# A graph network of two GATv2 layers and an edge attention: one-word sort records, part of them scattered later, and four buffers in the table loop

## The chip, the cores and the metric

The kernel runs on one core of one Trainium2 chip. The metric is the time of one execution in device microseconds (us). The program is one launch; it has no communication with other cores.

## What is computed

The graph has 6250 nodes with 128 features and 100000 edges (`src`, `dst`; `dst` is sorted). Cut to what matters:

```python
def _gatv2(x, edge_index, Wl, bl, Wr, br, att, bias):      # H = 3 heads of 128
    loops = jnp.arange(n)
    src = jnp.concatenate([edge_index[0], loops])
    dst = jnp.concatenate([edge_index[1], loops])
    xl = (x @ Wl + bl).reshape(n, h, d)
    xr = (x @ Wr + br).reshape(n, h, d)
    e = jax.nn.leaky_relu(xl[src] + xr[dst], NEG_SLOPE)
    score = jnp.einsum('ehd,hd->eh', e, att)
    ...
    alpha = ex / denom[dst]                                 # softmax over the edges of one dst
    out = jax.ops.segment_sum(alpha[:, :, None] * xl[src], dst, num_segments=n)

def _L0_gnn_ref(x, ...):
    x_in = _gatv2(x, edge_index, Wl1, ...)
    h = relu(_batchnorm(x_in @ W1 + b1, g1, be1))
    h2 = _gatv2(h, edge_index, Wl2, ...)
    return relu(_batchnorm(concat([h2, x_in]) @ W2 + b2, g2, be2))

def _L1_gnn_ref(embeds, ...):                               # 8 heads of 16
    q, k, v = rows @ qTrans, cols @ kTrans, cols @ vTrans   # rows = embeds[src], cols = embeds[dst]
    att = exp(clip(einsum('ehd,ehd->eh', q, k), -10, 10)); normalised over the edges of one src
    res = segment_sum(att * v, src) + embeds                # then a layer norm

x = x + _L0_gnn_ref(relu(layernorm(x)), ...)
x = x + _L1_gnn_ref(relu(layernorm(x)), ...)
```

The sums over edges run twice by `dst` (the two GATv2 layers) and once by `src` (the edge attention), so the edges are needed in both orders.

## The kernel before

Nodes lie in 49 blocks of 128 (`NB`). Edges are placed into slots so that each tile of 128 slots holds edges of one block alone; a table over the slots then says which row to gather (`gather_col` by `dst`, `gather_src` by `src`) and which node of the block (`lo`, the lane) each slot adds to. All edges are cut into 800 columns of 125 (`COLS`, `EC`). Each engine has its own instruction stream and queue; they meet at semaphores, and a block (`with nc.Block()`) ends with a barrier of all of them. The program is a chain of such stages:

- Constants, loading of the keys, and a counting loop.
- The sort block (`sort_by_dst`). First the rank loop works out the `dst` slot of each column on VectorE, ScalarE and TensorE. GpSimd (POOL) meanwhile writes one record of two words per edge with 800 indirect DMAs, one per column, into DRAM (`Records.write`, L634). After the rank loop the other engines go on without it: the ranks by `src` (`beside.on_vector` and its fellows), then `permute`, which puts the 800 columns into their `src` slots by one-hot products: VectorE makes two one-hots for a column (L795, L797), ScalarE scales the small one by two pieces of the record (L858), and TensorE adds four products of 416 columns to four banks (L837). Then come the load of x (L1010, L1012), a layer norm, and the tables of layer 1 (`table_parts`): 49 times TensorE multiplies a block, ScalarE copies it (L1169), SyncE stores it to `xl_table` (L1135), with two buffers in turn. The block ends when all of this and POOL's scatters are done.
- `slot_tables` reads the `dst` records back and makes the tables by `dst`.
- `gat_edges` of layer 1: 464 groups of two tiles. POOL gathers two times 128 rows of `xl_table` for a group (L1269), TensorE forms products (L1330, L1343), VectorE adds and takes the leaky relu (L1472, L1480), ScalarE sums scores (`reduce`, L1422) and weights rows (`weight`, L1406). The stream of each engine is a hardware loop over 16 groups (`pipeline`, L119), 25 times round in the middle. SyncE loads keys, gates, and an index tile for the gathers (`load_index`, L1288).
- `node_layer`, `batch_norm`, the tables of layer 2, `gat_edges` of layer 2, `node_layer`, `batch_norm` with a second load of x, `residual_tables` (stores to `kv_table`, L1794, four buffers), `edge_attention` (gathers by `gather_src`, L1914), and the end.

One fact of the compiled program, in which an instruction has 64 bytes: ScalarE's loop over 16 groups in `gat_edges` has 313 instructions, at positions 1058 to 1370 of its stream in layer 1 and 1999 to 2311 in layer 2. The functions that the change touches:

Of the kernel before, what the change touches and what calls it, by code (L numbers as in the profile page):

```python
# [5 lines left out]
F32 = mybir.dt.float32  # L6
# [26 lines left out]
MOVE = 8  # L33

PAD_KEY = 16384
# [4 lines left out]
G = 4  # L40
# [10 lines left out]
assert max(T_DST, T_SRC) <= TILES and GROUPS <= 512  # L51
# [87 lines left out]
class Core:  # L139


    def __init__(self, nc, ctx):
# [27 lines left out]
        self.block_row = sb("block_row", [1, TILES // G], I32)  # L170
# [10 lines left out]
        self.rec_d = dram("rec_by_dst", [SLOTS, 2], I32)  # L181
# [34 lines left out]
def constants(k, io, by_src):  # L216
# [4 lines left out]
    fill_d = cut(2 * SLOTROW, I32)  # L221
    node_f, long_i = cut(NB), cut(T_SRC, I32)
    made, filled, order, stored = k.sem("c_iota"), k.sem("c_fill"), k.sem("c_order"), k.sem("c_stored")
    with nc.Block() as block:
        @block.gpsimd
        def _(pool):
# [4 lines left out]
            nc.gpsimd.iota(long_i, pattern=[[1, T_SRC]], base=0, channel_multiplier=0).then_inc(made, 1)  # L231

        @block.vector
        def _(dve):
            do = Order(dve, order)
            do(nc.vector.memset(fill_d, 0))
            nc.vector.memset(fill_d.rearrange("p (s f) -> p s f", f=2)[:, :, 1:2], PAD_KEY).then_inc(filled, 1)
# [13 lines left out]
        @block.sync  # L251
        def _(sp):
            sp.wait_ge(filled, 1)
            sp.dma_start(k.rec_d.rearrange("(p s) f -> p (s f)", p=P), fill_d).then_inc(stored, 16)
            sp.wait_ge(stored, 16)


def sort_by_dst(k, io, beside):
# [23 lines left out]
    self_pos = far(NB, I32)  # L282
    self_rec = far(2 * NB, I32).rearrange("p (b f) -> p b f", f=2)
# [13 lines left out]
    records = Records(k, beside.pay)  # L297
# [11 lines left out]
    with nc.Block() as block:  # L309
# [9 lines left out]
        def _(dve):  # L319
# [13 lines left out]
            do(nc.vector.tensor_copy(beside.pay[:, :, 0], key["src"]))  # L333
            do(nc.vector.tensor_copy(beside.pay[:, :, 1], key["dst"]))
            do(nc.vector.tensor_copy(key_i, key["dst"]))
            do(nc.vector.tensor_scalar(part_i, key_i, P - 1, None, ALU.bitwise_and))
            do(nc.vector.tensor_copy(lo, part_i))
            do(nc.vector.tensor_scalar(part_i, key_i, 7, None, ALU.logical_shift_right))
            do(nc.vector.tensor_copy(hi, part_i))
            beside.key_blocks(do, key["src"])  # L340
# [54 lines left out]
    with nc.Block() as block:  # L395
        @block.vector
        def _(dve):
# [22 lines left out]
            do(nc.vector.tensor_copy(self_rec[:, :, 0], k.node_i[:, :]))  # L420
            do(nc.vector.tensor_copy(self_rec[:, :, 1], k.node_i[:, :]))
# [24 lines left out]
    move_on_vector, move_on_scalar, move_on_tensor, move_on_sync = beside.permute()  # L446
# [5 lines left out]
    with nc.Block() as block:  # L452
        @block.sync
        def _(sp):
# [11 lines left out]
            move_on_sync(sp)  # L466
# [5 lines left out]
        def _(act):  # L472
# [22 lines left out]
            pipeline(act, halves, [(1, round_table), (1, keep_rows), (1, mark_earlier)], R)  # L495
            beside.on_scalar(act, multiplied, halves)
            move_on_scalar(act)
# [5 lines left out]
        def _(pe):  # L503
# [51 lines left out]
            beside.on_tensor(pe)  # L555
# [60 lines left out]
class Records:  # L616
# [7 lines left out]
    def write(self, pool, ranked):  # L624
# [11 lines left out]
        for n in range(DEEP):  # L636
            pool.wait_ge(self.written[n], 16 * (COLS // DEEP))
# [1533 lines left out]
```

## Time and profile before

| | |
|---|---|
| time, median of 3 runs | 6332.61 us (6329.19 to 6332.86) |
| the profiled execution | 6359.09 us, span 6357.1 us |
| busy share of the span | PE 78%, DVE 85%, ACT 71%, POOL 62% |
| sort block (L452) | about 213 to 1533 us |
| `slot_tables` | 1533 to 1577 us |
| edges, layer 1 | 1577 to 3234 us |
| node layer, batch norm, tables of layer 2 | 3234 to 3442 us |
| edges, layer 2 | 3442 to 5036 us |
| node layer, batch norm, residual tables | 5036 to 5211 us |
| edge attention and the end | 5211 to 6357 us |

PE is TensorE, DVE is VectorE, ACT is ScalarE, POOL is GpSimd, SP is SyncE; a q behind a name is the engine's own queue of DMA issues and register work. No engine is busy throughout, so the question in each stage is which one ends it. "issue" as a releaser is time in which an engine waited for nothing that the profile shows.

### The profile page before, as it was taken

What the parts mean: (1) busy time and instruction counts of PE and PEld (TensorE: products, weight loads), DVE (VectorE), ACT (ScalarE), POOL (GpSimd) and SP (SyncE); (2) the same over time, 40 slices, a digit from 0 to 9 for tenths busy, and PEclk for the clock granted to TensorE, in tenths of its full rate; (3) what the DMA queues carried; (4) which work ended last, traced back from release to release, by engine and by line L of the source; (5) the groups of instructions that cost most, each with busy time, mean ns of one, the idle gap of its engine ahead of it and who ended that gap; (6) DMA issues with size and microseconds to landing.
All of it is one profiled execution on the core that took longest, in us unless ns stands there. A gap on an engine that the chain in (4) does not pass through costs nothing. (4 is left out here: it accounts for less than half of the span.)

```text
span 6357.1 us, 128308 instructions
## 1 busy us (share of the span) xinstructions
PE 4955.3 (78%) x23046; PEld 2929.5 (46%) x23047; DVE 5389.1 (85%) x12788; ACT 4531.1 (71%) x20210; POOL 3927.1 (62%) x3546
## 2 busy tenths in 40 slices
PE   3787799934888888888886999999999765666663
PEld 2564355512444444444463444444444455555552
DVE  9989988843999999999974999999999866666666
ACT  5577799921899999999844999999999753333332
POOL 0587777783666666666602666666666217777773
PEclk9999999968999999999998999999999977777776
DMA  0373000023555555555613555555555434444444
GB/s 13 59 73 38 2 1 2 2 38 85 149 136 137 138 137 138 138 136 138 132 24 121 143 143 142 143 143 144 142 142 142 68 96 128 129 128 128 127 129 77
DMA packets 352738, 655.93 MB, mean 103 GB/s; under 512 B 110151, under 2 KB 201221, under 8 KB 352116
## 3 DMA queue, kind: packets, MB, share of 16 engines
q0 software_dynamic: 185888, 481.62, 31.1%
q1 hardware_dynamic: 166612, 172.14, 12.0%
q14 instruction: 211, 1.73, 0.1%
q8 instruction: 27, 0.44, 0.0%
HBM read 617.73 MB, written 33.88 MB: 103 GB/s over the span
## 5 line engine op out<-in xcount | busy, mean ns | idle before, releaser
L1269 POOL DMA_INDIRECT feat_area<-xl_table,feat_area x1856 | 2090.3, 1126 | 1411.8 <-PE bank L1343 606.4
L1330 PE MATMUL bank<-node_area,feat_area 128*128 x3712 | 1470.4, 519 | 304.9 <-issue 136.0
L1406 ACT ACTIVATE feat_area<-feat_area 128x128 f32<-128x128 f32 x5104 | 1605.5, 419 | 78.1 <-issue 78.1
L1422 ACT ACTIVATE feat_area<-feat_area 128x130 f32<-128x130 f32 x5568 | 1498.6, 332 | 199.2 <-DVE feat_area L1480 197.4
L1343 PE MATMUL bank<-feat_area 128*128 128x390 f32 x3712 | 1402.2, 500 | 72.1 <-ACT feat_area L1406 47.3
L634 POOL DMA_INDIRECT rec_by_dst<-feat_area,gather_col x800 | 972.4, 1215 | 243.7 <-issue 232.4
L1914 POOL DMA_INDIRECT feat_area<-kv_table,gather_src x832 | 811.0, 975 | 464.1 <-issue 252.5
L1330 PEld LDWEIGHTS bank<-node_area,feat_area 128*128 128x128 f32 x3712 | 642.6, 191 | 922.1 <-issue 665.0
L1422 ACT ACTIVATION_READ_ACCUMULATOR feat_area<-feat_area 128x1 f32 x5568 | 1055.5, 190 | 0.0
L1343 PEld LDWEIGHTS bank<-feat_area 128*128 128x128 f32 x3712 | 680.6, 191 | 623.0 <-issue 227.5
L1472 DVE TENSOR_TENSOR feat_area<-bank,feat_area 128x780 f32<-128x780 f32 x928 | 887.5, 956 | 31.9 <-DMA feat_area<-xl_table,feat_area 29.8
L1480 DVE SCALAR_TENSOR_TENSOR feat_area<-feat_area 128x780 f32<-128x780 f32 x928 | 887.3, 956 | 0.0
L1954 PE MATMUL bank<-feat_area 128*128 128x136 f32 x1664 | 347.4, 370 | 415.2 <-DVE feat_area L2025 415.2
L837 PE MATMUL bank<-feat_area 125*128 125x416 f16 x3200 | 571.9, 340 | 8.5 <-ACT feat_area L858 8.5
L1967 ACT ACTIVATE feat_area<-feat_area 128x32 f32<-128x32 f32 x208 | 47.7, 229 | 737.6 <-DVE feat_area L2014 737.6
L858 ACT ACTIVATE feat_area<-feat_area 125x128 f16<-125x128 f16 x1600 | 514.5, 391 | 70.2 <-DVE feat_area L795 50.3
L1519 DVE SCALAR_TENSOR_TENSOR node_area<-node_area,stays,bank 128x390 f32 x812 | 495.1, 610 | 15.6 <-PE bank L1343 15.3
L1954 PEld LDWEIGHTS bank<-feat_area 128*128 128x128 f32 x1664 | 291.2, 255 | 467.8 <-DVE node_area L2040 322.0
L837 PEld LDWEIGHTS bank<-feat_area 125*128 125x128 f16 x3200 | 312.6, 98 | 267.7 <-DVE feat_area L797 9.0
L797 DVE TENSOR_SCALAR feat_area<-feat_area 125x832 f16<-125x832 f16 x800 | 408.6, 511 | 0.0
L2001 DVE TENSOR_TENSOR feat_area<-feat_area,bank 128x512 f32<-128x512 f32 x208 | 142.9, 687 | 293.5 <-DMA feat_area<-kv_table,gather_src 293.4
L1003 DVE TENSOR_TENSOR feat_area<-iota_f,lo_col 128x256 f32<-128x256 f32 x928 | 381.2, 411 | 0.0
(337 smaller groups left out, 6927.1 us busy)
## 6 DMA issues: line engine op xcount, KB each, us to landing
feat_area<-lo_slot SPq DMA_DIRECT2D x464, 128.0 KB, 3.3
feat_area<-xl_table,feat_area POOLq DMA_INDIRECT x1856, 3.5
feat_area<-lo_slot_src SPq DMA_DIRECT2D x104, 256.0 KB, 3.6
node_area<-lo_edge SPq DMA_DIRECT2D x100, 256.0 KB
xl_table<-feat_area SPq DMA_DIRECT2D x98, 195.0 KB, 2.4
feat_area<-kv_table,gather_src POOLq DMA_INDIRECT x832, 2.8
rec_by_dst<-feat_area,gather_col POOLq DMA_INDIRECT x800
feat_area<-gates SPq DMA_DIRECT2D x348, 32.0 KB
```

Of the source, the lines that this page charges most:

```text
L634: pool.indirect_dma_start(k.rec_d, bass.IndirectOffsetOnAxis(ap=self.pos[:, c:c + 1], axis=0), self.pay[:, c, :], None).then_inc(self.writ ...
L837: last = nc.tensor.matmul(out[n][m], self.to_lane[s][:, n * P:(n + 1) * P], self.to_tile[s][:, m * half:(m + 1) * half], start=False, stop ...
L858: last = nc.scalar.activation(self.to_lane[s][:, n * P:(n + 1) * P], self.at_lane[s], ACT.Copy, scale=self.piece[n][:, ds(c, 1)])
L1269: pool.indirect_dma_start(ring[:, at:at + HE], None, k.xl, bass.IndirectOffsetOnAxis(ap=index[s // CG][:, n:n + 1], axis=0)).then_inc(gath ...
L1330: last = nc.tensor.matmul(pair[s % 2][:, u, 0:HE], pick[s // 2 % 2][:, c:c + P], k.node[:, ds(columns[0], HE)], start=True, stop=True)
L1343: last = nc.tensor.matmul(sums_in[s % 2], place[s % 2][:, u * P:(u + 1) * P], ring[:, at:at + HE], start=u == 0, stop=u == GS - 1)
L1406: last = nc.scalar.activation(row[:, 0:D], row[:, 0:D], ACT.Copy, scale=row[:, D:D + 1])
L1422: last = nc.scalar.activation(at, at, ACT.Copy, accum_out=score_in[s // CG][:, to:to + 1])
L1472: nc.vector.tensor_tensor(z[s % V].rearrange("p (u e) -> p u e", u=GS), pair[s % 2][:, :, 0:HE], ring[:, s * W:(s + 1) * W].rearrange("p ( ...
L1480: nc.vector.scalar_tensor_tensor(out=zu, in0=zu, scalar=0.0, in1=att_w.unsqueeze(1).to_broadcast([P, GS, HE]), op0=ALU.max, op1=ALU.mult). ...
L1914: pool.indirect_dma_start(kv[s][:, u * KV:(u + 1) * KV], None, k.kv, bass.IndirectOffsetOnAxis(ap=rows, axis=0)).then_inc(gathered[s], 16)
L1954: last = nc.tensor.matmul(total[s % 2][u], place[s % 2][:, u * P:(u + 1) * P], wv[s % 2][:, u * VW:(u + 1) * VW], start=True, stop=True)
```

## The change

1. A record is one word (node times 256, plus lane plus 1). POOL scatters 640 of the 800 `dst` columns in the sort block. The other 160 go by one-hot products, with 464 columns a product instead of 416, straight behind the rank loop and ahead of the ranks by `src`.
2. Of the `src` columns 464 go by one-hot products; 336 are scattered by POOL, later: 16 in `slot_tables`, 64 in each `gat_edges`, 48 in each `node_layer`, 48 in the tables of layer 2 and the last 48 in `residual_tables`. Each such scatter waits for the one four before it (`LATE_DEEP`).
3. What `permute` did after its products (lanes, gather rows, seven turned tiles and their stores) is done in a new stage, `source_tables`, between `residual_tables` and `edge_attention`, which first loads both halves of the records and adds them.
4. In `gat_edges` POOL's loop is written out, and the gathers read their rows from `gather_col` itself; `load_index` and its tiles are gone.
5. `table_parts` has four buffers for staging, products and stores, and ScalarE stages a block two ahead.
6. `slot_tables` merges the two parts of the `dst` records, and takes the neighbours across partitions by two small products instead of two loads.

By the compiled program ScalarE's loop of 313 instructions stands at positions 1145 to 1457 in layer 1 now, and 2110 to 2422 in layer 2. The whole stream of POOL has 9725 instructions (4985 before).

The diff, cut to its core:

```diff
+DST_MOVED = 160
+SRC_MOVED = 464
+DST_WRITTEN = COLS - DST_MOVED
+SRC_WRITTEN = COLS - SRC_MOVED
+LATE_GAT = 64
+LATE_DEEP = 4
...
             pipeline(dve, halves, [(-1, read_table), (1, split_table), (2, key_columns), (-1, slots), (1, high_rows)], R)
+            dve.wait_ge(ranked, halves)
+            do = Order(dve, k.sem("r_order"))
+            do(nc.vector.memset(k.lo_col[:, T_DST:TILES], 0.0))
+            dst_moves.on_vector(dve, pos_d[:, DST_WRITTEN:], beside.word_dst[:, DST_WRITTEN:], k.lo_col[:, 0:T_DST])
             beside.on_vector(dve)
-            move_on_vector(dve)
+            src_moves.on_vector(dve, beside.pos_i[:, SRC_WRITTEN:], beside.word_src[:, SRC_WRITTEN:], beside.moved_i)
             dve.wait_ge(sorted_src, 1)
             norm_on_vector(dve)
...
     def write(self, pool, ranked):
-        for c in range(COLS):
+        for c in range(DST_WRITTEN):
...
+class LateWords:
+    def write(self, pool, n):
+        k = self.k
+        for c in range(self.done, min(self.done + n, SRC_WRITTEN)):
+            turn = c // LATE_DEEP
+            if turn:
+                pool.wait_ge(self.written[c % LATE_DEEP], 16 * turn)
+                pool.nop(nofuse=True)
+            pool.indirect_dma_start(k.word_s, bass.IndirectOffsetOnAxis(ap=self.slot[:, c:c + 1], axis=0),
+                                    self.word[:, c:c + 1], None).then_inc(self.written[c % LATE_DEEP], 16)
+            self.done = c + 1
...
+class Placement:
+    def on_vector(self, dve, pos, word, result):
...
+        pipeline(dve, n, [(0, shape)], MOVE, True)
+        dve.wait_ge(self.moved, n // 2)
+        for m in range(2):
+            to = slice(m * self.half, (m + 1) * self.half)
+            do(nc.vector.tensor_copy(self.low[:, to], self.out[1][m]))
+            do(nc.vector.scalar_tensor_tensor(out=result[:, to], in0=self.out[0][m], scalar=1024.0, in1=self.low[:, to],
+                                              op0=ALU.mult, op1=ALU.add))
+        dve.sem_inc(self.taken, 1)
...
+    def store(self, sp, table, result):
+        sp.wait_ge(self.taken, 1)
+        sp.dma_start(table, result).then_inc(self.stored, 16)
+        sp.wait_ge(self.stored, 16)
...
 def table_parts(...):
-    stage = [cut(P) for _ in range(2)]
-    out = [cut(gather_w) for _ in range(2)]
+    R = 4
+    stage = [cut(P) for _ in range(R)]
+    out = [cut(gather_w) for _ in range(R)]
...
-        pipeline(act, NB, [(1, take), (0, copy)])
+        pipeline(act, NB, [(2, take), (0, copy)], R)
...
 def gat_edges(...):
-            def gather(j, s):
-                g = U * j + s
-                pool.wait_ge(index_set[s // CG], 16 * j + 16)
-                if reused(j):
+            for g in range(groups):
+                s = g % U
+                if g >= U:
                     pool.wait_ge(summed, g - U + 1)
-                pool.nop(nofuse=True)
+                    pool.nop(nofuse=True)
                 for u in range(GS):
                     at = s * W + u * HE
-                    n = s % CG * GS + u
+                    rows = k.gather_col[:, g * GS + u:g * GS + u + 1]
                     pool.indirect_dma_start(ring[:, at:at + HE], None, k.xl,
-                                            bass.IndirectOffsetOnAxis(ap=index[s // CG][:, n:n + 1], axis=0)
-                                            ).then_inc(gathered[s], 16)
-            pipeline(pool, groups, [(0, gather)], U)
+                                            bass.IndirectOffsetOnAxis(ap=rows, axis=0)).then_inc(gathered[s], 16)
+                late.write(pool, (g + 1) * LATE_GAT // groups - g * LATE_GAT // groups)
...
-            pipeline(sp, groups, [(12, load_index), (8, load_keys), (0, load_gates)], U)
+            pipeline(sp, groups, [(8, load_keys), (0, load_gates)], U)
...
+def source_tables(k):
+            sp.dma_start(written, k.word_s.rearrange("(p t) o -> p (t o)", p=P)[:, 0:T_SRC]).then_inc(loaded, 16)
+            sp.dma_start(moved, k.moved_s).then_inc(loaded, 16)
...
+            dve.wait_ge(loaded, 32)
+            do(nc.vector.tensor_tensor(written, written, moved, ALU.add))
+            do(nc.vector.tensor_scalar(low_i, written, 255, None, ALU.bitwise_and))
+            do(nc.vector.tensor_copy(low_f, low_i))
+            nc.vector.tensor_scalar(k.lo_src[:, :], low_f, -1.0, None, ALU.add).then_inc(lo_set, 1)
+            do(nc.vector.tensor_scalar(k.gather_src[:, :], written, 8, None, ALU.logical_shift_right))
+            for n, row in enumerate(rows):
+                nc.vector.tensor_copy(row[0:t, :], k.bank[4 + n // 4][0:t, n % 4 * P:(n % 4 + 1) * P]).then_inc(rows_set, 1)
...
         residual_tables(k, io, scale[:, 0:1], shift[:, 0:1], x_loaded, h, q_area, late)
         k.recycle()
+        source_tables(k)
```

What stands on POOL's queue, from the first scatter of the sort block to the loop of layer 1's gathers, before (`rec_by_dst` is the table of records by `dst` in DRAM):

```order
L609 DMA rec_by_dst<-feat_area 131072x2 x49
L634 DMA rec_by_dst<-feat_area,gather_col 131072x2 x800
L452 UNCONDITIONAL_BRANCH
L1258 UNCONDITIONAL_BRANCH
L1269 DMA feat_area<-xl_table,feat_area 128x390 x32
L119 UNCONDITIONAL_BRANCH
L1264 REGISTER_ALU
L1269 DMA feat_area<-xl_table,feat_area 128x390 x2
```

And now, up to the second late scatter of layer 1 (`word_by_dst` and `word_by_src` are the tables of words):

```order
L622 DMA word_by_dst<-feat_area 131072x1 x49
L647 DMA word_by_dst<-feat_area,gather_col 131072x1 x640
L459 UNCONDITIONAL_BRANCH
L944 UNCONDITIONAL_BRANCH
L672 DMA word_by_src<-lo_src,gather_src 131072x1 x16
L943 UNCONDITIONAL_BRANCH
L1318 UNCONDITIONAL_BRANCH
L1328 DMA feat_area<-xl_table,gather_col 128x390 x16
L672 DMA word_by_src<-lo_src,gather_src 131072x1
L1328 DMA feat_area<-xl_table,gather_col 128x390 x14
L672 DMA word_by_src<-lo_src,gather_src 131072x1
```

160 scatters have left the sort block, 16 stand in `slot_tables`, and in the edges one scatter stands between each 14 or 16 gathers; the gathers name `gather_col`.

What VectorE has behind the last one-hot of `permute` (the branch closes the loop over columns), up to the layer norm, before:

```order
L119 COMPARE_AND_BRANCH
L804 CAST node_area<-bank 128x416 x2
L805 TENSOR_SCALAR node_area<-node_area 128x832
L806 TENSOR_SCALAR node_area<-node_area 128x832
L807 CAST node_area<-node_area 128x832
L808 TENSOR_SCALAR lo_src<-node_area 128x832
L809 CAST node_area<-node_area 128x832
L811 SCALAR_TENSOR_TENSOR gather_src<-bank,node_area 128x416 x2
L814 CAST node_area<-node_area 1x1024
L816 COPY node_area<-node_area 1x256
L818 SCALAR_TENSOR_TENSOR node_area<-node_area 1x256 x3
L820 CAST block_row<-node_area 1x256
```

And now, behind the one-hots of the `src` columns:

```order
L125 COMPARE_AND_BRANCH
L880 COPY node_area<-bank 128x416
L881 SCALAR_TENSOR_TENSOR feat_area<-bank,node_area 128x416
L880 COPY node_area<-bank 128x416
L881 SCALAR_TENSOR_TENSOR feat_area<-bank,node_area 128x416
L1134 MEMSET feat_area 128x128
L1076 TENSOR_REDUCE feat_area<-feat_area 128x49
```

Of the tail, four reads of the banks are left ahead of the norm; the rest is in `source_tables`. VectorE's rows behind the one-hots of the 160 `dst` columns, which stand in front of the ranks by `src` now (L685 is the first row of those ranks):

```order
L125 COMPARE_AND_BRANCH
L880 COPY node_area<-bank 128x464
L881 SCALAR_TENSOR_TENSOR lo_col<-bank,node_area 128x464
L880 COPY node_area<-bank 128x464
L881 SCALAR_TENSOR_TENSOR lo_col<-bank,node_area 128x464
L685 TENSOR_SCALAR feat_area<-bank 128x49
```

Nothing stood between the rank loop and L685's like before.

## Rows read from the trace of the kernel before

**Rows 1.** The page: the span, and each engine's busy time.

```profile
span 6357.1 us, 128308 instructions
...
PE 4955.3 (78%) x23046; PEld 2929.5 (46%) x23047; DVE 5389.1 (85%) x12788; ACT 4531.1 (71%) x20210; POOL 3927.1 (62%) x3546
```

**Rows 2.** Busy time by stretch: window, its length, then each engine's busy us.

```profile
core 0: us, PE busy (x) PEld busy (x) DVE busy (x) ACT busy (x) POOL busy (x), PEclk, DMA share, GB/s
...
900.00:1000.00 100.00, 100.00 (x564) 54.81 (x563) 88.14 (x282) 90.23 (x282) 79.59 (x68) 1.00 0.08 2
...
1500.00:1533.00 33.00, 25.79 (x72) 12.49 (x70) 10.15 (x18) 12.74 (x36) 0.00 (x0) 0.99 0.34 121
...
3600.00:5000.00 1400.00, 1266.00 (x3742) 629.41 (x3742) 1380.56 (x2911) 1345.62 (x7432) 945.64 (x831) 1.00 0.57 142
```

**Rows 3.** Groups of instructions, 720 to 1310 us: busy and mean; idle before.

```profile
L837 PE MATMUL bank<-feat_area 125*128 125x416 f16 x3200 | 571.9, 340 | 8.5 <-ACT feat_area L858 8.5
L858 ACT ACTIVATE feat_area<-feat_area 125x128 f16<-125x128 f16 x1600 | 514.5, 391 | 70.2 <-DVE feat_area L795 50.3
L634 POOL DMA_INDIRECT rec_by_dst<-feat_area,gather_col x393 | 470.8, 1198 | 119.7 <-issue 119.4 <-DMA rec_by_dst<-feat_area,gather_col 0.3
```

**Rows 4.** Timeline of VectorE at the end of `permute`: start, us, instruction, idle before.

```profile
1294.10 1.22 DVE L804 CAST node_area<-bank 128x416 int32<-128x416 f32 x2 [4.37 <-PE bank L837]
...
1340.91 6.69 DVE L1020 TENSOR_REDUCE feat_area<-feat_area 128x49 f32<-128x6272 f32 x1 [29.48 <-DMA feat_area<-in_x]
```

**Rows 5.** Timeline of SyncE's queue, 1300 to 1540 us.

```profile
1312.39 18.10 SPq L1012 DMA_DIRECT2D feat_area<-in_x  x1
...
1409.31 121.77 SPq L1135 DMA_DIRECT2D xl_table<-feat_area  x49
```

**Rows 6.** Timeline of SyncE's queue and VectorE at the second load of x.

```profile
5117.71 8.76 SPq L1012 DMA_DIRECT2D feat_area<-in_x  x1
...
5131.65 0.49 DVE L1849 TENSOR_TENSOR feat_area<-bank,feat_area 128x128 f32<-128x128 f32 x2 [5.50 <-DMA feat_area<-in_x]
```

**Rows 7.** DMA issues of the table loop, 1409 to 1500 us, then 1508 to 1532.

```profile
xl_table<-feat_area SPq DMA_DIRECT2D x30, 195.0 KB, 5.4
...
xl_table<-feat_area SPq DMA_DIRECT2D x16, 195.0 KB, 2.3
```

**Rows 8.** ScalarE's waits and instruction packets, 1600 to 3100, then 3500 to 4900 us.

```profile
ACT feat_area L1406 <- issue: 67.6, 25, 3.3
...
q14 instruction: 134, 1.10, 0.3%
...
ACT feat_area L1406 <- issue: 5.5, 24, 0.2
...
q14 instruction: 10, 0.08, 0.0%
```

**Rows 9.** POOL: waits 3500 to 4900 us, then its timeline around 1498 us.

```profile
POOL feat_area L1269 <- PE bank L1343: 237.8, 229, 2.3
...
1497.70 1.18 POOL L634 DMA_INDIRECT rec_by_dst<-feat_area,gather_col  x1 [0.30 <-issue]
1582.48 0.99 POOL L1269 DMA_INDIRECT feat_area<-xl_table,feat_area  x1 [83.60 <-DMA feat_area<-gather_col]
```

**Rows 10.** Timeline of SyncE's queue: first issues of later stages, and table stores.

```profile
1576.68 0.40 SPq L1277 DMA_DIRECT2D feat_area<-in_L_gnn_att  x1
...
3234.39 0.35 SPq L1633 DMA_DIRECT2D feat_area<-in_L_gnn_bl  x1
...
3364.94 74.79 SPq L1135 DMA_DIRECT2D xl_table<-feat_area  x49
3442.26 0.41 SPq L1277 DMA_DIRECT2D feat_area<-in_L_gnn_att  x1
...
5036.39 0.35 SPq L1633 DMA_DIRECT2D feat_area<-in_L_gnn_bl  x1
...
5159.28 45.06 SPq L1794 DMA_DIRECT2D kv_table<-feat_area  x49
```

More of the change, by code:

```diff
@@ L253, in _ @@
             sp.wait_ge(filled, 1)
-            sp.dma_start(k.rec_d.rearrange("(p s) f -> p (s f)", p=P), fill_d).then_inc(stored, 16)
-            sp.wait_ge(stored, 16)
+            for words in (k.word_d, k.word_s):
+                sp.dma_start(words.rearrange("(p s) f -> p (s f)", p=P), fill).then_inc(stored, 16)
+            sp.wait_ge(stored, 32)
 def sort_by_dst(k, io, beside):
@@ L465, in _ @@
             beside.on_sync(sp)
-            move_on_sync(sp)
+            src_moves.store(sp, k.moved_s, beside.moved_i)
             sp.sem_inc(sorted_src, 1)
@@ L971, in _ @@
         def _(pe):
+            tiles = k.lo_col[:, :].rearrange("p (t g) -> p g t", g=TG)
+            for half in range(2):
+                for u in range(4):
+                    last = nc.tensor.transpose(k.bank[5 + half][:, u * P:(u + 1) * P], tiles[:, 4 * half + u, :], k.ident[:, :])
+                last.then_inc(words, 1)
+            pe.wait_ge(keys_set, 1)
+            nc.tensor.matmul(k.bank[7][:, 0:1], down, key_f[:, SLOTROW - 1:SLOTROW], start=True, stop=True)
+            nc.tensor.matmul(k.bank[7][:, 1:2], up, key_f[:, 0:1], start=True, stop=True).then_inc(edges, 1)
             pe.wait_ge(rows_ready, 1)
@@ L980, in _ @@
             nc.tensor.matmul(k.bank[4][:, 0:GROUPS], k.ones[0:1, :], stay, start=True, stop=True).then_inc(spread, 1)
-def block_words(k, engine, word, n):
-    return k.nc.values_load_multi_w_load_instructions(
-        k.block_row[0:1, ds(word, n)], engines=(engine,), min_val=0, max_val=(1 << G * BLOCK_BITS) - 1,
-        skip_runtime_bounds_check_because="every block was limited to NB - 1 before it was packed")[1]
-def block_columns(eng, packed, tiles, width):
-    blocks = [((packed >> (BLOCK_BITS * u)) & ((1 << BLOCK_BITS) - 1)).with_bounds(min_val=0, max_val=NB - 1) for u in tiles]
-    return [eng.snap(b * width) for b in blocks]
 def key_rows(k, out, lo_col, tile, n):
@@ L1207, in node_tables, with gat_edges @@
         block.vector(on_vector)
[L1210 removed]
+def gat_edges(k, att, tag, late):
     nc = k.nc
@@ L1222, in gat_edges @@
     lo_bc = [cut(GS * P, BF16) for _ in range(2)]
-    index = [cut(CT, I32) for _ in range(2)]
     att_w = cut(HE)
@@ L1786, in residual_tables, with _ @@
     with nc.Block() as block:
+        @block.gpsimd
+        def _(pool):
+            late.write(pool, COLS)
+            late.wait(pool)
         @block.sync
```

430 lines of the change are left out of this document (232 added, 198 removed).

## The prediction

> **What bounds the kernel now.** I read the page first. Its span is 6357.1 us, and no engine fills it: VectorE is busy for 85%, TensorE for 78% [rows 1]. So I went stage by stage through the busy times by stretch, and in each stage asked which wait ends last.
>
> In `permute` TensorE is busy 100.00 of 100 us, with 564 matmuls, four to a column: 0.709 us a column [rows 2]. It hardly waits (8.5 us in all), while ScalarE takes two times 0.391 us and stays just behind it [rows 3]. POOL scatters alongside, one column in (470.8 + 119.7) / 393 = 1.50 us [rows 3], and goes on to 1498.9 [rows 9]. That overlaps all that follows `permute`: the tail from 1294.10, the load of x, for which VectorE waits 29.48 us [rows 4], and the table loop, whose 49 stores stretch over 121.77 us [rows 5]. In it a store of 195 KB lands after 5.4 us while POOL scatters and after 2.3 us once it has ended [rows 7]. The same loop in layer 2, without POOL, takes 74.79 us [rows 10].
>
> The edge stages are two runs of one program, from 1576.68 to 3234.39 (1657.7 us) and from 3442.26 to 5036.39 (1594.1 us) [rows 10]. They differ by 63.6 us. ScalarE's waits tell why: 25 times it stands at L1406, the first work of a round of its loop, for nothing but "issue", 67.6 us in layer 1 against 5.5 in layer 2, and the instruction packets number 134 against 10 [rows 8]. ScalarE fetches its loop anew in each round of layer 1. VectorE then sits at 1380.56 of 1400 us in layer 2 [rows 2]; with the stall gone it is the bound. POOL has slack: 237.8 us of waits for a free place in the ring in 1400 us of layer 2 [rows 9].
>
> **The sort block.** The 160 `dst` columns go by products of 464 columns in place of 416. TensorE's pace scales to 0.709 x 464/416 = 0.791 us, so 160 cost +127. Around them stand one more drain (4.37 before L804 [rows 4]), four bank reads of 0.61, and setup on 160 columns: +10. Packing words adds about ten operations of some 0.6 us (that of a bank read), less two copies and a smaller fill: +3. The 336 `src` columns that are taken out save 336 x 0.709 = -238, and the setup on 464 in place of 800 columns -4.
>
> The tail was 1294.10 to 1312.4, when x was being asked for [rows 4, 5]: 18 us. Now four bank reads (2.4), then SyncE stores 425 KB and waits for it; 195 KB land in 2.3 [rows 7], so I take 4.5. That is 7 with handovers: -11.
>
> POOL has 160 scatters fewer, 240 us at 1.50, and ends near 1258 instead of 1498.9. The moves end 102 us earlier by the terms above (+127 +10 +3 -238 -4), at 1192, and the tail at 1199. So POOL still scatters through the load of x and part of the norm, but has ended when the table loop begins, near 1409 - 113 = 1296. The load of x therefore keeps its price here (29.48), where the later one, with no scatters, is worked off in 5131.65 - 5116.9 = 15 us [rows 6]; I count nothing for it, and -12 stays as a bound. The table loop is free of scatters. It then goes at the slower of landing over buffers (2.3/4) and TensorE, which was busy 25.79 us for 18 blocks after POOL had ended [rows 2], 1.4 us a block: 49 x 1.4 = 68 against 121.77, and the first store comes a little earlier: -55.
>
> Sum of the block: +127 +10 +3 -238 -4 -11 -55 = -168. POOL no longer ends last anywhere in it.
>
> **`slot_tables` and layer 1's edges.** In `slot_tables` VectorE gets eight more operations on 1024 columns, about 0.7 each by their size, and loses two loads: +4. In the edges the first gather came at 1582.48, behind the load of its index [rows 9], and the block began at 1576.7 [rows 10]; now it can start at once: -5. The fetch stall depends on where the loop stands. Packets have 1.10 MB / 134 = 8.2 KB, 128 instructions. A body of 313 touches three such pieces or four. The one at 1058 (34 past a multiple of 128) stalls, the one at 1999 (79 past) does not. If four pieces are what stalls, the edge of the pieces lies between 35 and 79, and a body is free if it starts at most 71 behind an edge. Layer 1's new place, 1145 (121 past), is free for edges from 50 on. Layer 2's, 2110 (62 past), is free for edges up to 62. The moments of the packets inside a round, which no view groups, favour an edge near 61; they move my chances, not the sum. So layer 1 saves 67.6 - 5.5 = -62.
>
> The page "Runtime: NRT & Kernel Launch" of the Trainium skill, section "Instruction fetch mechanics", gives a window of two pages of 256 instructions, outside which a taken branch stalls. By a count from zero layer 1's old loop would lie in two such pages and layer 2's in three, so the stall would be in layer 2; the trace has it in layer 1. With an unknown offset the rule makes the new loop of layer 2 stall for about half of the offsets that fit; the sum by it would be 61 us higher (the rival below). By the same section unrolling POOL's loop does no harm; 800 scatters written out show a gap of 0.30 us each [rows 9].
>
> **Late scatters.** POOL needs 2 x (945.64/831 + 0.26) = 2.8 us for a group's two gathers [rows 2, 9] (213.5 us of short gaps over 831, about 0.26 each), against a group's 1594.1/464 = 3.44. One scatter of 1.5 comes in each 7.25 groups, whose slack is 4.4 us. Hidden, but DMA and a nearly full engine disturb: +2 in each edge stage. The start of layer 2 gains its index load too: -5. Node layers: 48 scatters are 72 us, in stages of 80 to 100 us with little traffic: +2 in all. Tables of layer 2: now 48 scatters beside 49 stores of 5.4 [rows 7]; with four buffers and a copy and a wake-up 6.3/4 = 1.6 a block, as against 74.79/49 = 1.53 [rows 10]: 0, within -8 (TensorE's 1.4) and +8. Residual tables had 45.06 us for 49 stores [rows 10], 0.92 a block, with four buffers already; a landing of 5 us makes that about 1.2 until POOL is done: +10.
>
> **`source_tables`.** A barrier, two loads of 425 KB (5), five operations of 0.6 to 0.8 (4), turned tiles, seven row copies, stores and their landing (6), a barrier: +16.
>
> **Sum.** -168 +4 -5 -62 +2 (layer 1) -3 (layer 2) +2 +0 +10 +16 = -204. Against the profiled execution's 6359.1 that is 6155. That execution lay 26.5 us above the median of the runs, and the change acts on both alike: 6332.6 - 204 = 6129.
>
> **The rivals.**
> - *Layer 2's edge loop takes the stall over.* For it: its start lies one instruction inside the free stretch by my edge, and 17 of the 45 possible edges make it stall. Against it: the packets' moments. It costs what layer 1 lost, +62: 6191.
> - *Layer 1 keeps its stall*, by an edge below 50: 6129 + 62 = 6191 too.
> - *The load of x is faster and the tables of layer 2 reach TensorE's pace*: -12 and -8, 6109. It needs POOL's scatters to end sooner than 1258, or to weigh less as one word.
> - *Slower than before: POOL becomes the bound of the edges.* Place: the gathers of both layers, now written out and with waits on the ring and a scatter among them. A group has 3.44 - 2.8 - 0.2 = 0.43 us of slack with the scatters in. Beyond it each 0.1 us a gather costs 2 x 0.1 x 928 groups = 186 us. The gain of 204 is gone once a gather takes 0.22 + 0.11 = 0.33 us more than its 1.4. At 0.35 more the time is 6129 + (0.70 - 0.43) x 928 = 6380. For it: POOL's program doubles to 9725 instructions, and its gathers grow from 0.99 at the start to 1.14 under load [rows 2, 9]. Against it: the scatters written out keep their gap of 0.30.
> - *The four buffers do nothing*: the gain is then what the end of the scatters gives, 1.5 a block in place of 1.4, +5: inside the range of my own case.
>
> By the page "DMA: Bandwidth & Descriptors" of the Trainium skill, section "SWDGE vs HWDGE vs iDMA", each DMA engine goes round between POOL's queue and SyncE's. The two landings above, 5.4 and 2.3 us, agree; it is what speaks against scatters beside the residual stores.
>
> **Chances and range.** My case 0.66, its own range 6105 to 6150; layer 2's stall 0.18; layer 1's 0.06; load of x and tables faster 0.06; POOL as the bound 0.04. The range reaches from 6085, past the fourth case, over both stall cases to 6200. A measurement of this kernel can tell 0.2%, 13 us, from no change. Faster has every case but POOL's, which at its break-even would give no change: 0.95; same 0.01; slower 0.04. The case of the buffers is inside the first.
>
> **What would show it.** Right: the sort block ends near 1365; POOL's last scatter in it near 1258; the table loop's stores stretch over some 70 us; "issue" ahead of ScalarE's `weight` under 10 us in both layers, and few instruction packets; both edge stages near 1595; POOL's waits on the ring smaller but there; residual stores near 55 us. Wrong: over 100 instruction packets in an edge stage, POOL without waits on the ring, one-hot columns above 0.8 us for `dst`, or VectorE ending them.

## The result: slower by 2%

The changed kernel takes 6462.88 us (median of 4 runs, 6441.73 to 6473.54) against 6332.55 us: a ratio of 1.0204, with a 95% interval from 1.0192 to 1.0216. The forecast had it faster by 3%. Of the six runs of the last kernel in experiment 4 one took 8766.65 us, at a mean granted clock of 0.764 instead of 0.92, and it is left out there. The page of the changed kernel says how the engines stand over the whole span:

```profile
span 6460.5 us, 122307 instructions
...
PE 4903.6 (76%) x22358; PEld 2913.7 (45%) x22359; DVE 5302.3 (82%) x12461; ACT 4437.2 (69%) x19858; POOL 4239.2 (66%) x3722
```

The span is 103.4 us longer than in [rows 1], with less work on VectorE. SyncE's queue shows at which stage the time went. These are the load of x, the first issues of the stages, and between them the table stores with the time over which they stretch:

```profile
1344.69 8.39 SPq L1068 DMA_DIRECT2D feat_area<-in_x  x1
...
1426.67 64.29 SPq L1192 DMA_DIRECT2D xl_table<-feat_area  x49
...
1542.07 0.40 SPq L1334 DMA_DIRECT2D feat_area<-in_L_gnn_att  x1
...
3159.36 0.35 SPq L1685 DMA_DIRECT2D feat_area<-in_L_gnn_bl  x1
...
3291.89 63.54 SPq L1192 DMA_DIRECT2D xl_table<-feat_area  x49
3357.50 0.40 SPq L1334 DMA_DIRECT2D feat_area<-in_L_gnn_att  x1
...
5129.14 0.35 SPq L1685 DMA_DIRECT2D feat_area<-in_L_gnn_bl  x1
...
5252.41 45.16 SPq L1851 DMA_DIRECT2D kv_table<-feat_area  x49
5305.42 0.32 SPq L1949 DMA_DIRECT2D feat_area<-word_by_src  x1
...
5319.08 0.25 SPq L2021 DMA_DIRECT2D feat_area<-block_s  x1
```

Against [rows 5] and [rows 10], in profiled time:

| stretch | before | predicted | measured |
|---|---|---|---|
| start of the program to the first issue of layer 1's edges | 1576.7 | 1412.7 | 1542.1 |
| edges, layer 1 | 1657.7 | 1592.7 | 1617.3 |
| from there to layer 2's edges | 207.9 | 208.9 | 198.1 |
| edges, layer 2 | 1594.1 | 1591.1 | 1771.6 |
| from there to `source_tables` (to `edge_attention` before) | 174.9 | 186 | 176.3 |
| `source_tables` | - | 16 | 13.7 |

Two stretches carry nearly all of the miss: +129 us ahead of layer 1's edges, and +180 us in layer 2's. Layer 1's edges add 25, and experiment 3 takes them up.

**The rank loop.** The row of the reduction that ends each half of four columns (VectorE, 200 times, with the start of the first and the last) gives the length of the loop. Before:

```profile
L595 DVE TENSOR_REDUCE gather_col<-node_area x200: 336/349/358, 223.9 to 560.3; 125x196 f32 x88, 125x4 int32<-125x196 f32 x12
```

and after:

```profile
L604 DVE TENSOR_REDUCE gather_col<-node_area x200: 337/350/358, 225.4 to 709.5; 125x196 f32 x88, 125x4 int32<-125x196 f32 x12
```

This instruction takes no longer (349 and 350 ns in the middle), and yet the loop ends at 709.5 instead of 560.3, 149 us later. The edit has hardly touched the loop itself. What it shares with the edit is the DMA engines, on which the keys come in (`lo_edge`) while POOL scatters. The DMA view of 300 to 500 us follows; there q1 carries SyncE's loads of keys. Before:

```profile
DMA packets 12098, 14.90 MB, mean 75 GB/s; under 512 B 4964, under 2 KB 4964, under 8 KB 12096
...
q1 hardware_dynamic: 8017, 14.61, 70.5%
...
node_area<-lo_edge SPq DMA_DIRECT2D x55, 256.0 KB
```

and after:

```profile
DMA packets 9399, 9.83 MB, mean 49 GB/s; under 512 B 4711, under 2 KB 4711, under 8 KB 9397
...
q1 hardware_dynamic: 5275, 9.60, 68.4%
...
node_area<-lo_edge SPq DMA_DIRECT2D x38, 256.0 KB
```

38 loads of keys instead of 55, two thirds of the bytes, and the queue is as busy for it (68.4 against 70.5%). The engines stand for some microseconds at a time. One such moment, from the timeline of all engines:

```profile
341.14 0.22 PE L531 MATMUL bank<-node_area 128*128 128x128 f16 x1 [1.36 <-issue]
...
343.40 0.26 PE L531 MATMUL bank<-node_area 128*128 128x128 f16 x1 [2.05 <-issue]
...
345.38 0.59 ACT L493 CAST node_area<-bank 128x512 bf16<-128x512 f32 x1 [7.25 <-remote]
...
346.16 0.36 DVE L598 TENSOR_TENSOR node_area<-bank,node_area 125x196 f32<-125x196 f32 x1 [6.71 <-remote]
```

TensorE stops inside a batch of four products that have no wait between them, and ScalarE and VectorE then wait 7 us. TensorE's granted clock falls with it. Its busy time, as the third number, and its mean granted clock, third from the end, over the loop before and after:

```profile
225.00:561.00 336.00, 305.36 (x5133) 238.60 (x5130) 296.46 (x989) 257.38 (x591) 268.33 (x223) 0.96 0.64 76
...
225.00:710.00 485.00, 361.92 (x5161) 276.27 (x5159) 301.45 (x993) 262.25 (x593) 386.57 (x324) 0.80 0.75 53
```

In the changed kernel the clock is 1.00 from 250 to 275 us, with TensorE busy for 24.96 us of the 25. From 275 to 300 us, in which POOL's first scatter of a column falls (284.4), TensorE is busy for 22.23 us, at 0.93; from 300 to 325 us for 16.84 us, at 0.74, so that part of the stretch is at the lower of the clock's two levels. About as many products (5161 and 5133 in the records) keep TensorE busy 57 us longer, and it is idle 92 us longer. How much the standing still would cost without the lower clock, no run separates.

**Layer 2's edges.** ScalarE's waits at the first work of its loop, and the instruction packets, in layer 1 (1600 to 3100 us) and in layer 2 (3500 to 5000 us):

```profile
ACT feat_area L1454 <- issue: 5.5, 26, 0.2
...
q14 instruction: 21, 0.17, 0.0%
...
ACT feat_area L1454 <- issue: 129.7, 50, 3.6
...
q14 instruction: 136, 1.11, 0.2%
```

Layer 1 has lost its stall, 67.6 to 5.5 us [rows 8], and layer 2 has taken it over, twice as long. The timeline of ScalarE and VectorE at one turn of the loop shows why it is twice:

```profile
3833.97 0.40 ACT L1454 ACTIVATE feat_area<-feat_area 128x128 f32<-128x128 f32 x1 [2.55 <-issue]
...
3836.60 1.57 ACT L1454 ACTIVATE feat_area<-feat_area 128x128 f32<-128x128 f32 x5 [2.23 <-issue]
...
3841.54 0.35 DVE L1611 SCALAR_TENSOR_TENSOR feat_area<-feat_area,bank 51x128 f32<-51x128 f32 x1 [4.98 <-PE bank L1421]
```

There are two waits of 2.55 and 2.23 us, one operation apart. VectorE, which was the bound, waits 4.98 us for a product of TensorE behind them.

### The profile page after: what moved, and what is told of

Read it like the earlier page. It is cut to its first block and busy times, and to the rows that moved or that the text cites. A ratio compares the mean times of both kernels' runs of the same rounds, so it can differ in the third digit from the quotient of the medians.

```text
span 6460.5 us, 122307 instructions
## 1 busy us (share of the span) xinstructions
PE 4903.6 (76%) x22358; PEld 2913.7 (45%) x22359; DVE 5302.3 (82%) x12461; ACT 4437.2 (69%) x19858; POOL 4239.2 (66%) x3722
## 5 line engine op out<-in xcount | busy, mean ns | idle before, releaser
L1328 POOL DMA_INDIRECT feat_area<-xl_table,gather_col x1856 | 2156.9, 1162 | 958.4 <-issue 532.2
L1391 PE MATMUL bank<-feat_area 128*128 128x390 f32 x3712 | 1432.0, 509 | 135.1 <-ACT feat_area L1454 92.6
L1391 PEld LDWEIGHTS bank<-feat_area 128*128 128x128 f32 x3712 | 694.2, 194 | 688.9 <-issue 286.3
L647 POOL DMA_INDIRECT word_by_dst<-feat_area,gather_col x640 | 773.6, 1209 | 195.0 <-issue 167.9
L672 POOL DMA_INDIRECT word_by_src<-lo_src,gather_src x336 | 448.0, 1333 | 476.0 <-ACTq L943 241.1
L2056 PEld LDWEIGHTS bank<-feat_area 128*128 128x128 f32 x1664 | 301.1, 263 | 474.2 <-DVE node_area L2142 324.1
L897 PE MATMUL bank<-feat_area 125*128 125x416 f16 (+1 forms) x2496 | 459.6, 346 | 6.7 <-ACT feat_area L913 4.5
L913 ACT ACTIVATE feat_area<-feat_area 125x128 f16<-125x128 f16 x1248 | 398.9, 390 | 74.3 <-DVE feat_area L871 53.6
L897 PEld LDWEIGHTS bank<-feat_area 125*128 125x128 f16 x2496 | 243.5, 98 | 223.6 <-DVE feat_area L873 8.9
```

What stands on the lines that cost most here:

```text
L647: pool.indirect_dma_start(k.word_d, bass.IndirectOffsetOnAxis(ap=self.pos[:, c:c + 1], axis=0), self.word[:, c:c + 1], None).then_inc(self ...
L897: last = nc.tensor.matmul(self.out[p][m], sh.to_lane[s][:, p * P:(p + 1) * P], sh.to_tile[s][:, m * half:(m + 1) * half], start=False, sto ...
L1328: pool.indirect_dma_start(ring[:, at:at + HE], None, k.xl, bass.IndirectOffsetOnAxis(ap=rows, axis=0)).then_inc(gathered[s], 16)
L1391: last = nc.tensor.matmul(sums_in[s % 2], place[s % 2][:, u * P:(u + 1) * P], ring[:, at:at + HE], start=u == 0, stop=u == GS - 1)
L2056: last = nc.tensor.matmul(total[s % 2][u], place[s % 2][:, u * P:(u + 1) * P], wv[s % 2][:, u * VW:(u + 1) * VW], start=True, stop=True)
```

## The experiments

### 1. Where ScalarE's loop stands

The same edit shifts the loop of either kernel: n tiny copies at the head of ScalarE's program of one layer's edges.

```diff
         def _(act):
+            for i in range({"1": 28, "2": 0}[str(tag)]):
+                nc.scalar.copy(k.filler[0:1, i:i + 1], k.ones[0:1, i:i + 1])
+
             def exps(j, s):
```

The kernel before, with 28 copies in layer 1:

> The kernel before, with 28 tiny copies put in front of ScalarE's program of the layer 1 edges, so that its loop of 313 instructions starts at 1086 (62 past a multiple of 128, the place that layer 2's loop has in the changed kernel) instead of 1058; layer 2's moves to 2027 (107 past). Theory of the fetch by place: layer 1 now stands twice a round for instructions, as layer 2 does in the changed kernel, about 130 us of issue ahead of weight, and the stage grows from 1658 to about 1770 us; layer 2 stays near 1594; time about 6333 + 115 = 6448 us. Rival, that the long stage in the changed kernel comes from the written-out gathers or the late scatters: layer 1 keeps its 1658 us and the time 6335 to 6345 us.

Measured: 6453.73 us, ratio 1.0175 (1.0158 to 1.0192). Its layer 1 takes 1767.0 us, its layer 2 1593.3. The waits at `weight` and the packets, 1600 to 3100 us:

```profile
ACT feat_area L1410 <- issue: 129.9, 46, 3.4
...
q14 instruction: 126, 1.03, 0.2%
```

The waits are those of the changed kernel's layer 2 (129.9 and 129.7 us), with no late scatter and no written-out loop in the program. The rival falls.

The changed kernel, with 10 copies in layer 2:

> The changed kernel, with 10 tiny copies in front of ScalarE's program of the layer 2 edges, so that its loop starts at 2120 (72 past a multiple of 128) instead of 2110 (62 past). Theory of the fetch by place: issue ahead of weight under 10 us in both layers, under 30 instruction packets in layer 2, the stage of layer 2 from 1773 down to about 1600 us, time about 6463 - 170 = 6293 us. Rival, that the late scatters and the written-out gathers make layer 2 long: no change, 6463 us.

Measured: 6331.88 us, against 6343.41 of the kernel before on the same chip (ratio 0.9987, 0.9975 to 0.9999). Layer 2's edges take 1622.8 us instead of 1771.6, with 5.5 us of issue. Ten copies bring the ratio from 1.0204 to 0.9987. But 1622.8 is not the 1600 that was expected, nor the 1594.1 of the kernel before; experiment 3 takes that up.

The kernel before, with 40, 30 and 16 copies in layer 1:

> The kernel before with 40 tiny copies in front of ScalarE's program of the layer 1 edges, so that its loops start at 1098 (74 past a multiple of 128) and 2039 (119 past). Theory of the fetch by place: both loops are free of the wait, layer 1 falls from 1658 to about 1595 us, layer 2 stays at 1594, time about 6333 - 62 = 6271 us. Rival, that layer 1 is longer for another reason (its cold tables, its first rounds): no change, 6335 us.

Measured: 6282.07 us, ratio 0.9913 (0.9896 to 0.9929). Layer 1 takes 1592.3 us, layer 2 1591.0: the stall was all of the 63.6 us between the layers.

> The kernel before with ScalarE's layer 1 loop at 1088, 64 past a multiple of 128, two instructions further than in the run that stalled twice. Theory: the pieces begin at 63 or 64, so this start is free: under 10 us of issue, stage near 1593 us. Rival, that they begin further on (up to 71): two waits a round again, stage near 1767 us.

Measured, in one run: 6276.56 us, layer 1 1593.7 us. The waits and packets of the run:

```profile
ACT feat_area L1410 <- issue: 5.8, 27, 0.3
...
q14 instruction: 12, 0.10, 0.0%
```

> The kernel before with ScalarE's layer 1 loop at 1074, 50 past a multiple of 128: some 13 instructions of the body lie ahead of the first edge, against 29 at the old place and 1 or 2 at 1086. Theory (the fetch of the second piece overlaps with what the first holds): the loss per round lies between the 2.5 us of the old place and the 7 us of 1086, and the stage between 1658 and 1767 us. Rival, that only a nearly empty first piece stalls twice: stage near 1658 us.

Measured, in one run: 6349.31 us, layer 1 1670.5 us. The waits and packets:

```profile
ACT feat_area L1410 <- issue: 67.2, 25, 3.5
ACT feat_area L1426 <- issue: 19.5, 25, 1.6
...
q14 instruction: 135, 1.11, 0.2%
```

The wait at L1410 is that of the old place (67.2 against 67.6), and a second of 0.8 us has come up at L1426. By start modulo 128: 34 loses 2.5 us a round, 50 loses 3.1, 62 about 7 (6 in the changed kernel), and 64, 72, 74, 79, 107, 119 and 121 lose nothing. So, if the pieces have 128 instructions, an edge of them lies at 63 or 64, and the loss grows the fewer instructions of the body stand ahead of the first such edge. A reading that fits, and that no run shows by itself: the first wait is for the piece that the branch goes back to; what stands in it covers the fetch of the next, and with one or two instructions in it nothing is covered.

### 2. What slows the rank loop

The place of the tables in DRAM:

```diff
-        self.word_d = dram("word_by_dst", [SLOTS, 1], I32)
-        self.word_s = dram("word_by_src", [P * TILES, 1], I32)
-        self.moved_s = dram("moved_by_src", [P, T_SRC], I32)
+        self.word_d = dram("word_by_dst", [2 * SLOTS, 1], I32)[0:SLOTS, :]
         self.lo_edge = dram("lo_edge", [COLS * P], F16)
...
         self.rowgates = dram("rowgates", [2, TILES], F32)
+        self.word_s = dram("word_by_src", [P * TILES, 1], I32)
+        self.moved_s = dram("moved_by_src", [P, T_SRC], I32)
```

> The changed kernel, with the words by dst and the keys (lo_edge) at the DRAM offsets that the records and the keys have in the kernel before (81920 and 1130496), and the two new tables behind all others. Theory of the place in DRAM: the rank loop, which now ends near 710 us instead of 560, goes back to about 560, and the time falls by about 150 to 6313 us. Rival, that one word of 4 bytes a record is what disturbs the loads of keys: no change, rank loop to 710, 6463 us.

Measured: 6494.56 us, ratio 1.0234 (1.0209 to 1.0258). The row of the reduction ends where it did in the changed kernel:

```profile
L604 DVE TENSOR_REDUCE gather_col<-node_area x200: 336/348/358, 225.9 to 710.0; 125x196 f32 x88, 125x4 int32<-125x196 f32 x12
```

The place is not it. The size of the record (only the core of the edit is shown):

```diff
-        self.word_d = dram("word_by_dst", [SLOTS, 1], I32)
+        self.word_d = dram("word_by_dst", [SLOTS, 2], I32)
...
-                                    self.word[:, c:c + 1], None).then_inc(self.written[n], 16)
+                                    self.word[:, c, :], None).then_inc(self.written[n], 16)
...
-            do(nc.vector.tensor_copy(word_f, raw))
+            do(nc.vector.tensor_copy(word_f, pairs.rearrange("p (s f) -> p s f", f=2)[:, :, 0]))
```

> The changed kernel, with records by dst of two words (8 bytes, the second unused) again, everything else as changed; lo_edge stands at offset 2080768. Theory of the word size: the rank loop ends near 560 us again and the time falls by about 145, to 6318 us (one more copy and a larger read in slot_tables cost about 3). Rival, the place in DRAM: not what it was before either, so the rank loop may stay long, 6466 us.

Measured: 6335.98 us against 6343.41 (ratio 0.9985, 0.9975 to 0.9994), and the loop ends at 554.8:

```profile
L606 DVE TENSOR_REDUCE gather_col<-node_area x200: 336/339/357, 229.9 to 554.8; 125x196 f32 x88, 125x4 int32<-125x196 f32 x12
```

Layer 1's edges begin at 1401.6 instead of 1542.1; the prediction had 1412.7. So the second word, which nobody reads, brings the ratio from 1.0204 to 0.9985. TensorE's clock over this loop is 0.99 again. Is it the size of a write, or how close the writes lie?

```diff
-        self.word_d = dram("word_by_dst", [SLOTS, 1], I32)
+        self.word_d = dram("word_by_dst", [2 * SLOTS, 1], I32)
...
+                dve.wait_ge(summed, h + 1)
+                nc.vector.tensor_scalar(records.pos[:, ds(HALF * h, HALF)], pos_d[:, ds(HALF * h, HALF)], 2, None,
+                                        ALU.mult).then_inc(ranked, 1)
```

> The changed kernel, with words of 4 bytes by dst at every second word of a table twice as large: VectorE writes doubled slots beside the slots (one small operation more per half of a quartet of columns). Theory of the crowded table (neighbouring words that fall into one piece of memory): the rank loop ends near 570 to 590 us. Rival, that a write of 4 bytes itself is what is slow, wherever it goes: it ends near 710 us or later, as in the changed kernel.

Measured, in one run: 6380.25 us, and the loop ends at 605.1:

```profile
L605 DVE TENSOR_REDUCE gather_col<-node_area x200: 337/351/358, 228.6 to 605.1; 125x196 f32 x88, 125x4 int32<-125x196 f32 x12
```

That is 15 us past the range that was expected. The operation that doubles a slot takes 0.17 us and stands 200 times in the loop: up to 34 us of the 50 that it is longer than with pairs. The standing is gone too:

```profile
225.00:606.00 381.00, 334.87 (x5195) 238.35 (x5193) 334.77 (x1197) 267.98 (x599) 301.79 (x260) 0.99 0.47 67
```

TensorE's clock is 0.99, its waits for nothing but "issue" from 300 to 500 us are 2.1 us (35.6 in the changed kernel, 2.8 with pairs, 8.5 in the kernel before), and 52 loads of keys come in, against 38. So 4-byte writes at a distance of 8 bytes do little harm to this loop. Writes into a table half as large, where neighbouring slots lie 4 bytes apart, cost over 100 us. As the edges are sorted by `dst`, the 125 words of one scattered column go to slots next to each other, so these writes are close in time as well. That the loads of keys and TensorE itself stand still in such moments is seen, and not explained: no run here shows what they wait for.

### 3. The late scatters

```diff
-LATE_GAT = 64
+LATE_GAT = 0
```

> The changed kernel with the 10 copies and with no late scatter in the edge stages: the 128 that stood there are written in the residual tables' stage, which gets longer by some 190 us. Only the edge stages are looked at; with the scatters they take 1621 and 1623 us. Theory of the late scatters: both fall to about 1595 us, as layer 2 was before. Rival, that the written-out gathers cost it: they stay near 1620 us.

Measured, in one run: edges 1588.5 us in layer 1 and 1591.2 in layer 2, against 1620.6 and 1622.8 with the scatters. 64 scatters cost 32 us in each layer; the written-out gathers cost nothing, and layer 1 even gains the few microseconds of the index load. The whole run (6454.36 us) has the scatters elsewhere. What they do stands in the waits of VectorE's first addition, 1700 to 3000 us, here with them (the run of both mends, below):

```profile
L1527 DVE TENSOR_TENSOR feat_area<-bank,feat_area 128x780 f32<-128x780 f32 x378 | 362.8, 960 | 27.0 <-DMA feat_area<-xl_table,gather_col 23.2 <-ACT feat_area L1477 2.2 <-PE bank L1382 1.3
```

and without:

```profile
L1524 DVE TENSOR_TENSOR feat_area<-bank,feat_area 128x780 f32<-128x780 f32 x388 | 372.4, 960 | 2.3 <-DMA feat_area<-xl_table,gather_col 1.7 <-PE bank L1379 0.5
```

23.2 against 1.7 us of waits for a gather. POOL's own rows of the run with the scatters, in the same stretch:

```profile
L1332 POOL DMA_INDIRECT feat_area<-xl_table,gather_col x753 | 881.8, 1171 | 318.8 <-issue 215.7 <-PE bank L1395 103.1
L675 POOL DMA_INDIRECT word_by_src<-lo_src,gather_src x52 | 78.5, 1509 | 15.8 <-issue 13.4 <-PE bank L1395 2.4
```

A scatter takes 1.51 us and 0.30 of gap here, 1.8 in place of the 1.5 of the sort block. POOL still waits 103.1 us for a free place in the ring (209.6 without the scatters). So it had slack on average, and still gathers are late at times.

### 4. Both mends, and what is best

The changed kernel with records of two words and ten copies:

> The changed kernel with both mends: records by dst of two words, and 10 tiny copies ahead of ScalarE's program of the layer 2 edges. Theory (word size and place of the loop add up): 6463 - 127 - 131 = 6205 us, rank loop to 560 us, both edge stages near 1620 us. Rival, that the two share a cause: nearer 6320 us.

Measured: 6176.43 us against 6339.83, ratio 0.974 (0.9724 to 0.9756). That is 29 us below the 6205 that was expected. Each mend keeps its whole gain beside the other, so the two causes are separate and add up; where the 29 us come from no run shows. With two buffers in the table loops again:

> The changed kernel with both mends, and two buffers in the table loops as before, ScalarE one block ahead; 58 tiny copies keep the layer 2 loop at 2120. Theory of the buffers: the stores of layer 1's tables stretch over 75 us instead of 64 and those of layer 2, beside 48 scatters, over 120 us instead of 64; 6176 + 10 + 55 = 6240 us. Rival, that four buffers are worth little, because a landing takes 2.3 us in either: 6195 us.

Measured: 6182.72 us against 6335.70, ratio 0.9753 (0.9739 to 0.9767). The stores of layer 1's tables stretch over 72.5 us instead of 64.8, and those of layer 2, beside the 48 late scatters, over as little:

```profile
3158.78 72.04 SPq L1196 DMA_DIRECT2D xl_table<-feat_area  x49
```

So the theory falls (6240 us, and 120 us for the stores of layer 2), and the rival stands. Two more buffers are worth 8 us a loop in these rows, and 6176 and 6183 can hardly be told apart. A landing takes 2.2 us there, not 5.4. With no scatter in the edges, 64 more columns by one-hot products, and 64 scatters at the end of the sort block:

```diff
-LATE_GAT = 64
+LATE_GAT = 0
-SRC_MOVED = 464
+SRC_MOVED = 528
...
             beside.on_vector(dve)
+            dve.sem_inc(late_ready, 1)
...
             pool.wait_ge(scattered, 16 * NB)
+            pool.wait_ge(late_ready, 1)
+            late.write(pool, 64)
```

> The changed kernel with both mends, and no scatter in the edge stages: 64 more src columns go by one-hot products (528 of 800), and 64 of the 272 scattered ones are written at the end of the sort block, behind the dst scatters. Each edge stage should fall by about 32 us (as it did when the late scatters were taken out), 64 columns cost 64 x 0.71 = 45 us, and the scatters beside the tables of layer 1 up to 8: 6176 - 64 + 45 + 8 = 6165 us, between 6150 and 6185. Rival, that the scatters in the sort block hold the load of x and the table loop as in the kernel before: 6200 us or more.

Measured: 6151.14 us, the middle one of five runs, against 6335.70, ratio 0.9705 (0.9693 to 0.9718). Its edges take 1590.3 and 1585.4 us. It beats both kernels. The 64 scatters by `src` run beside layer 1's table stores and hold them up by nothing (64.29 us in the changed kernel, without scatters):

```profile
1326.82 63.84 SPq L1199 DMA_DIRECT2D xl_table<-feat_area  x49
```

## Why the prediction was wrong

Three terms failed, and all in the same direction: the scatters of one word, which had no term, cost 149 us in the rank loop; layer 2's edges, counted as free of the fetch stall, took 149 us of it; and the late scatters, +2 in each layer, cost 32.

**The word.** The step "Packing words adds about ten operations" counted what VectorE does for a word, and took the scatter itself as unchanged: POOL's 1.50 us a column, which it was. That scatters of half the size could disturb the loads of the rank loop was neither a term nor a rival. It cost 149 us there. The trace of before had the question in it: scatters by `dst` made a store land after 5.4 us instead of 2.3 [rows 7], and I read that as the price of any scatter. It is a price of the scatters by `dst`, and it was there with records of two words already: these spare the rank loop, and not the stores. The words by `src` have 4 bytes and slots 4 bytes apart too, but a column of them does not go to neighbouring slots, as the edges are not sorted by `src`. That this is what makes them harmless is likely, and no run changes it alone. Beside the tables of layer 2 they left the landing as it was:

```profile
xl_table<-feat_area SPq DMA_DIRECT2D x46, 195.0 KB, 2.2
```

With that, my +10 for the residual stores (45.16 us, as the 45.06 before) and my 0 for the tables of layer 2 (63.54, where TensorE's pace gives 68) were wrong in the other direction, by 10 and 11 us. The two landings in the prediction, 5.4 and 2.3 us, therefore do not show that sharing the DMA engines with POOL is what slows a store: here POOL scatters too, and the landing is 2.2 us.

**The fetch.** "A body is free if it starts at most 71 behind an edge" holds for every start that was tried (the furthest is 57 or 58 behind one), and so does the range 35 to 79 for the edge. "The moments of the packets ... favour an edge near 61" failed: it is 63 or 64, two or three instructions off. The chance of 0.18 was the choice that decided, where the bare range gave 17 in 45. The rival's price was wrong too. "It costs what layer 1 lost, +62" took one wait a round for the stall, and a start just ahead of an edge has two: 129.7 us of issue, and 1771.6 - 1622.8 = 149 us of the stage; the 4.98 us that VectorE waits at one turn show the way that it takes through TensorE. The rule of two pages of 256, in "Runtime: NRT & Kernel Launch" of the Trainium skill, section "Instruction fetch mechanics", had layer 2's new loop stall for half of the offsets; it was right in the outcome. With pages counted from 64 it fits every start above as well as my pieces of 128 do; no run has a start that would tell the two apart.

**The late scatters.** "+2 in each edge stage" was 32. I weighed POOL's mean slack of 4.4 us over 7.25 groups against a scatter of 1.5. Slack on average does not stop a single gather from being late. The working has a slip as well: (3.44 - 2.8) x 7.25 is 4.6, not 4.4. It decides nothing.

**What held.** The 160 `dst` columns and their setup: 137 us forecast, and from the end of the rank loop at 709.5 to the first row of the ranks by `src` it is 137. That row, the row of all one-hot products, and that of POOL's scatters by `dst`:

```profile
846.47 0.21 DVE L685 TENSOR_SCALAR feat_area<-bank 128x49 int32<-128x49 f32 x1 [0.85 <-PE bank L800]
...
L897 PE MATMUL bank<-feat_area x2496: 336/340/591, 714.5 to 1337.6; 125*128 125x416 f16 x142, 125*128 125x464 f16 x50
...
L647 POOL DMA_INDIRECT word_by_dst<-feat_area,gather_col x640: 1175/1184/1392, 284.4 to 1251.6; - x160
```

POOL's last scatter stands at 1251.6 (forecast 1258). Layer 1's table stores stretch over 64.29 us (68), and layer 1's issue waits are gone. The load of x was costed as unchanged on the ground that POOL would still scatter. As the rank loop had made everything late, it did not, and VectorE waited half as long as in [rows 4]. Its first read of a bank and that wait:

```profile
1337.94 0.59 DVE L880 COPY node_area<-bank 128x416 f32<-128x416 f32 x1 [4.36 <-PE bank L897]
...
1358.45 6.69 DVE L1076 TENSOR_REDUCE feat_area<-feat_area 128x49 f32<-128x6272 f32 x1 [14.77 <-DMA feat_area<-in_x]
```

From the bank's read at 1337.94 to the load at 1344.69 it is 6.8 us (forecast 7 for the tail). With pairs, where POOL does scatter then, the wait for x is 23.98 us.

## What to carry to other kernels

A table that is filled by scattered DMA writes can be too dense where the writes of one scatter land side by side: ask which do, and what else is being loaded or stored in those microseconds; here 4 unread bytes a record are worth 2%. An edit that only adds instructions on an engine moves every later loop of that engine against the pieces in which its instructions are fetched. Look for "issue" at the first work of each round and for the count of instruction packets, and shift the loop by a few instructions where they are there. Before believing a mean slack, look at what is queued behind the thing that is put in.

## What the runs showed that was not expected

A start two instructions further on (62 to 64 past a multiple of 128) changes a loop of 25 rounds by 173 us. A loop with one or two instructions ahead of the edge waits twice a round, one with 13 or 14 waits 2.7 and 0.8 us, one with 29 or 30 waits once. Scatters by `dst` of 4-byte words at 4 bytes' distance hold up loads of 256 KB on the other queue, 38 in 200 us instead of 55, and TensorE with them, whose granted clock goes from 0.96 to 0.80 over the loop; the same words at 8 bytes' distance let 52 loads through, at 0.99. Words of 4 bytes by `src`, scattered beside stores of 195 KB, cost these nothing (63.84 us for 49), while records of 8 bytes by `dst` stretched them to 121.77 us.
